# Another order of the same instructions in the six attention layers: feed-forward matmuls between scores and values on TensorE, query copy ahead of the exponentials, key scaling first on GpSimd

## What is computed

```python
for i in range(DEPTH):          # 6 layers
    x = attn_layer(shift_tokens(x), Wqkv[i], q_scale[i], k_scale[i], Wo[i]) + x
    x = ffn_layer(shift_tokens(x), ln_g[i], ln_b[i], W1[i], b1[i], W2[i], b2[i]) + x

# attn_layer
q, k, v = split(x @ Wqkv)                    # 128 -> 3 * 1024
q, k = l2norm(q) * qs, l2norm(k) * ksc       # per head of 64
q = q*cos*scale + rotate_half(q)*sin*scale   # k the same with 1/scale
sim = q @ k2.T * 8                           # own window of 32 keys and the one before
out = softmax(mask(sim)) @ v2
return out @ Wo                              # 1024 -> 128

# ffn_layer (hidden width 341)
a, gate = split(layernorm(x) @ W1 + b1)
return a * gelu(gate) @ W2 + b2
```

## Time and profile before

| | |
|---|---|
| median of three runs | 4083.23 us |
| the profiled execution | 4075.82 us |
| its span, first to last instruction | 4074.0 us |
| granted TensorE clock, mean | 0.976 |
| TensorE matmuls busy | 3730.5 us (92%) |
| VectorE busy | 3452.1 us (85%) |
| ScalarE busy | 3408.5 us (84%) |
| GpSimd busy | 2380.0 us (58%) |

### The profile page before, as it was taken

One profiled execution on the slowest core, in us unless ns is written; L12 is line 12 of the kernel. 1 busy time (PEld: TensorE's weight loads), 2 busy tenths in 40 slices (PEclk: granted clock), 3 DMA queues, 4 the chain that ended last, 5 costly groups with the idle time before them and its releaser, 6 DMA issues.

```text
span 4074.0 us, 125302 instructions
## 1 busy us (share of the span) xinstructions
PE 3730.5 (92%) x49248; PEld 2372.9 (58%) x49248; DVE 3452.1 (85%) x7192; ACT 3408.5 (84%) x9269; POOL 2380.0 (58%) x1420
## 2 busy tenths in 40 slices
PE   5999999967999999999999998999989999999997
PEld 2444444434666666666666666666666666666664
DVE  6999999957888888888878888888888888988884
ACT  3999999946888888888888888888888888888885
POOL 2434434436667666666666666666666666666662
PEclk8999999978999999999999999999999999999998
DMA  1000001002333333333333333333333333433332
GB/s 49 7 11 9 9 9 36 1 2 52 81 76 80 85 83 87 76 77 84 86 77 72 80 86 84 83 77 74 76 95 80 77 78 73 98 79 82 75 83 57
DMA packets 158791, 263.19 MB, mean 65 GB/s; under 512 B 45696, under 2 KB 72064, under 8 KB 157952
## 3 DMA queue, kind: packets, MB, share of 16 engines
q1 hardware_dynamic: 158208, 255.20, 26.6%
HBM read 26.43 MB, written 2.10 MB: 7 GB/s over the span
## 4 chain that ended last, share of the span: by engine, by line
PE 66%; ACT 13%; DVE 11%; issue 8%; POOL 1%; SPq 1%; DMA 1%; DVEq 0%; ACTq 0%; POOLq 0%
PE ps L655 18%; PE ps L724 7%; ACT arena L930 7%; PE ps L601 5%; PE ps L596 5%; PE ps L709 5%; PE ps L542 4%; PE ps L733 4%; PE ps L688 4%; PE ps L768 3%; PE ps L762 3%; PE ps L537 3%; DVE arena L1146 2%; PE ps L775 2%; ACT arena L917 2%
## 5 line engine op out<-in xcount | busy, mean ns | idle before, releaser
L655 PE MATMUL ps<-WB,arena 128*128 128x512 f32 x2304 | 1087.4, 606 | 46.9 <-ACT arena L946 27.0
L930 ACT ACTIVATE arena<-arena,nmx 128x64 f32<-128x64 f32 x3072 | 1022.1, 340 | 3.9 <-DVE arena L1221 3.3
L475 POOL TENSOR_TENSOR arena<-arena 128x1024 f32<-128x1024 f32 x192 | 455.2, 2371 | 476.0 <-DVE arena L1146 476.0
L655 PEld LDWEIGHTS ps<-WB,arena 128*128 128x128 f32 x2304 | 415.6, 193 | 471.8 <-issue 456.1
L484 POOL TENSOR_TENSOR arena<-arena,rr 128x1024 f32<-128x1024 f32 x192 | 367.3, 1913 | 524.7 <-DVE rr L1215 524.7
L1140 DVE TENSOR_TENSOR arena<-ps,tables 128x1024 f32<-128x1024 f32 x384 | 463.9, 1208 | 177.8 <-ACT arena L906 177.6
L906 ACT ACTIVATE arena<-ps 128x1024 f32<-128x1024 f32 x384 | 393.2, 1024 | 252.8 <-PE ps L655 247.1
L930 ACT ACTIVATION_READ_ACCUMULATOR arena<-arena,nmx 128x1 f32 x3072 | 594.5, 194 | 0.0
L724 PE MATMUL ps<-arena 128*64 128x64 f32 x12288 | 445.8, 231 | 117.4 <-issue 97.8
L724 PEld LDWEIGHTS ps<-arena 128*64 128x64 f32 x12288 | 409.4, 144 | 180.3 <-issue 168.8
L1146 DVE TENSOR_TENSOR arena<-ps,tables 128x512 f32<-128x512 f32 x768 | 489.5, 677 | 0.0
(11 more groups left out here) (109 smaller groups left out, 6482.1 us busy)
## 6 DMA issues: line engine op xcount, KB each, us to landing
arena<-arena SPq DMA_DIRECT2D x768, 128.0 KB, 2.3
arena<-arena SPq DMA_DIRECT2D x1536, 64.0 KB
WB<-wb SPq DMA_DIRECT2D x24, 512.0 KB, 4.6
arena<-X SPq DMA_DIRECT2D x384, 32.0 KB, 1.9
arena<-Y SPq DMA_DIRECT2D x96, 128.0 KB, 2.3
arena<-wa SPq DMA_DIRECT2D x8, 581.0 KB, 3.7
WF<-wf SPq DMA_DIRECT2D x6, 537.5 KB, 4.1
keep<-xT SPq DMA_DIRECT2D x1, 2048.0 KB, 7.8
```

Source lines behind the costliest of these rows:

```text
L475: pool.tensor_tensor(tu[:, K], t1[:, K], t2[:, K], ALU.add).then_inc(addk_r, 1)
L655: i = pe.matmul(banks[:, c, :], xs_[t % RING], WB[:, w * INNER + c * COL:w * INNER + (c + 1) * COL], start=True, stop=True)
L930: i = act.activation(pe3[:, :, h, :], sc[:, 64 * h:64 * h + 64].rearrange("p (k q) -> p k q", k=2), ACT.Exp, bias=nmx[:, h:h + 1], accum_o ...
```

## The change

The orders within the step are rewritten for TensorE, ScalarE, VectorE and GpSimd. No instruction is added or removed, and none changes its size. On TensorE the key transposes go between the projections of keys and queries, the query transposes ahead of the output projection, `scores` directly behind `values_of`, and `ff_back`, the first gate and value matmul, and `ff_down` between `scores` and `attend`. On ScalarE the copy of the turned keys goes between the two squares, and that of the turned queries ahead of all 16 exponentials; `ff_norm` stands ahead of the last GELU's place. On VectorE `norms` goes ahead of `ff_stats`, `masked` ahead of `inverse`, `ff_final` and `ff_hidden` are spread between them, and `ff_unit` goes behind `maxima`. On GpSimd `unit_k` goes ahead of `ff_rstd` and `probs_norm`. SyncE's order stays.

```diff
--- before.py
+++ after.py
@@ -505,12 +505,12 @@
                 if live(s + 1):
                     add_k(s + 1)
                     add_q(s + 1)
+                    unit_k(s + 1)
                 if chunk(s, 7) is not None:
                     ff_rstd(chunk(s, 7))
                 if live(s - 1):
                     probs_norm(s - 1)
                 if live(s + 1):
-                    unit_k(s + 1)
                     unit_q(s + 1)
 
 
@@ -779,24 +779,27 @@
             for s in range(-2, TILES + LAG):
                 if live(s + 1):
                     keys_of(s + 1)
+                if live(s):
+                    turn_k(s)
+                if live(s + 1):
                     queries_of(s + 1)
                 if live(s):
-                    turn_k(s)
+                    turn_q(s)
                 if live(s - 3):
                     output(s - 3)
                 if live(s):
-                    turn_q(s)
                     values_of(s)
+                if chunk(s, 7) is not None:
+                    ff_turn(s, chunk(s, 7))
+                if live(s):
+                    scores(s)
+                if chunk(s, 8) is not None:
+                    ff_back(s, chunk(s, 8))
+                if chunk(s, 9) is not None:
+                    ff_gate(s, chunk(s, 9), 0)
+                    ff_value(chunk(s, 9), 0)
                 if chunk(s, 10) is not None:
                     ff_down(s, chunk(s, 10))
-                if chunk(s, 7) is not None:
-                    ff_turn(s, chunk(s, 7))
-                if chunk(s, 9) is not None:
-                    ff_gate(s, chunk(s, 9), 0)
-                if live(s):
-                    scores(s)
-                if chunk(s, 9) is not None:
-                    ff_value(chunk(s, 9), 0)
                 if live(s - 2):
                     attend(s - 2)
                 if chunk(s, 9) is not None:
@@ -804,8 +807,6 @@
                     ff_value(chunk(s, 9), 1)
                     ff_gate(s, chunk(s, 9), 2)
                     ff_value(chunk(s, 9), 2)
-                if chunk(s, 8) is not None:
-                    ff_back(s, chunk(s, 8))
 
 
         @block.scalar
@@ -964,15 +965,15 @@
             for s in range(-2, TILES + LAG):
                 if live(s + 1):
                     square(s + 1, kv_ps, K, k_mm, sqk_r)
+                if live(s):
+                    turned_k(s)
+                if live(s + 1):
                     square(s + 1, q_ps, Q, q_mm, sqq_r)
                 if live(s):
-                    turned_k(s)
+                    turned_q(s)
                 if live(s - 1):
                     exponents(s - 1, range(0, 4))
                     exponents(s - 1, range(4, 8))
-                if live(s):
-                    turned_q(s)
-                if live(s - 1):
                     exponents(s - 1, range(8, 12))
                     exponents(s - 1, range(12, 16))
                 if chunk(s, 9) is not None:
@@ -983,10 +984,10 @@
                     ff_gelu(chunk(s, 9), 1)
                 if live(s):
                     values(s, 1)
+                if chunk(s, 8) is not None:
+                    ff_norm(chunk(s, 8))
                 if chunk(s, 9) is not None:
                     ff_gelu(chunk(s, 9), 2)
-                if chunk(s, 8) is not None:
-                    ff_norm(chunk(s, 8))
                 if live(s - 2):
                     outputs(s - 2)
                 if 0 < s + 1 < TILES:
@@ -1277,25 +1278,25 @@
                     residual(s - 3)
                 if live(s + 1):
                     sumsq(s + 1)
+                    norms(s + 1)
                 if chunk(s, 7) is not None:
                     ff_stats(chunk(s, 7))
-                if live(s + 1):
-                    norms(s + 1)
+                if chunk(s, 9) is not None:
+                    ff_hidden(chunk(s, 9), 0)
+                if live(s):
+                    masked(s)
+                if live(s - 1):
+                    inverse(s - 1)
+                if chunk(s, 9) is not None:
+                    ff_hidden(chunk(s, 9), 1)
                 if chunk(s, 10) is not None:
                     ff_final(chunk(s, 10))
+                if live(s):
+                    maxima(s)
                 if chunk(s, 9) is not None:
-                    ff_hidden(chunk(s, 9), 0)
-                if live(s - 1):
-                    inverse(s - 1)
-                if live(s):
-                    masked(s)
+                    ff_hidden(chunk(s, 9), 2)
                 if chunk(s, 7) is not None:
                     ff_unit(chunk(s, 7))
-                if chunk(s, 9) is not None:
-                    ff_hidden(chunk(s, 9), 1)
-                    ff_hidden(chunk(s, 9), 2)
-                if live(s):
-                    maxima(s)
                 q = chunk(s, 11)
                 if q is not None and q >= FF - NT // PER:
                     final(q)
```

## The result

The changed kernel takes 4047.61 us (median of 7 runs, 4042.57 to 4050.83), the kernel before 4080.06 us in the 7 runs beside it (4064.23 to 4088.86). The ratio is 0.9926, 95% interval 0.9908 to 0.9945: 0.7% faster, some 30 us. The forecast was 4097 us, slower. The time lies within the range, on the other side of no change, and a rival was nearest: "Program text wins", 4066 us, down to 4045. A ratio of 0.9926 with this interval is a gain clear of noise, though a small one.

A forecast was written before the change was run, and what follows sets the result against it. Each step was taken to have its own limit (TensorE's matmul sum in the gate step), plus waits for program text. Terms 18 - 24 - 4 + 18 + 5 = +13 us; forecast 4083 + 14 = 4097 us, range 4045 to 4132.

The forecast's parts named there:

- Program text wins: Rival, faster: stop relief reaches the back step too, `scores` gets no more stops; 4066 us, down to 4045; chance 0.28.
- First term: Plain down and turn steps: `turned_k` leaves the chain; 15.23 instead of 15.29 us, 13.91 instead of 13.93, -0.08 together.
- Fifth term: `scores` in down and gate steps: without `ff_down` and `ff_gate` ahead, stops for program text rise, +18 us.
- Fourth term: `attend`: matmuls between it and `scores` give program text time to come; -24 us in down steps, -4 in gate steps.
- relief in the back step: Rival's claim for `attend` in back steps: of 29.1 us of stops, 0.55 us of each goes, 12 us.
- Second term: Back step: `queries_of` waits 1.1 us for the later `ff_unit` instead of 0.28; +0.45 us a step.
- 40 us or more: Sign expected in the new profile: TensorE's total wait on the line of `ff_unit`, 9.1 us before.
- Third term: Gate step: `unit_k` ahead of `probs_norm` on GpSimd delays `unit_q`, so TensorE waits; +0.35 us a step.
- Sixth term: First step of each layer, bound by VectorE until `ff_unit`: `maxima` ahead costs 1.12 us, five times, +5 us.

## Why the prediction was wrong

**First term, the chain of the plain step: right.** 15.23 and 13.91 us were forecast, 15.26 and 13.90 came. Its last sentence was wrong: that the earlier query copy "makes `scores` ready sooner, for which nothing critical waits".

**Fifth term, stops in `scores` (+18 us): the step that failed.** They were to rise by 18 us and fell by 37.6. I took the number of instructions ahead of `scores` for the cause and the back step's row for its size. What the runs show in its place is the query copy. ScalarE's copy before and after, and TensorE's down step after, beside the earlier trace rows:

```profile
1538.98 1.00 ACT L922 ACTIVATE arena<-ps 128x1024 f32<-128x1024 f32 x1
1532.41 1.02 ACT L923 ACTIVATE arena<-ps 128x1024 f32<-128x1024 f32 x1
1535.76 1.61 PE L709 MATMUL ps<-arena 64*32 64x64 f32 x128
1537.30 2.84 PE L775 MATMUL ps<-arena,WF 128*128 128x512 f32 x6
```

Before, the copy ended at 1539.98 and `scores` started at 1540.78, behind the last matmul of `ff_down`: until 1539.98 TensorE's sequencer stood at the wait of `scores`, though the engine had work. Now the copy ended at 1533.43, 2.3 us ahead of `scores`, and the sequencer can run ahead into the next block of program text while the matmuls before it are still at work. The runs bear out that the copy decides: with it late, `scores` stops for 41.8 us (before), 41.3, 37.5 and 14.6 us; with it early, in all the others, for 2.6 to 5.7 us, whether `ff_down` stands ahead (3.4 us) or not.

The trace also holds the start of every packet of the instruction queue, and these show when a block is asked for. In the kernel before, at 20 of the 22 stops in `scores` the packet that the stop waited for started 1.04 to 1.84 us behind the end of the query copy (at the other two 0.14 and 0.37 us ahead of it); at the 165 places where `scores` went on into a new block without a stop, it had started 1.55 us or more ahead of the end of the copy. With the copy between the exponentials, all 7 packets started 1.13 to 1.49 us behind it. So a sequencer held at a wait asks for its next block late. What stays open is why the 14.6 us are so few: they fall only where `scores` starts 1 to 11 instructions behind the start of a block, and in the kernel before 1 to 56. Something else in the new TensorE order narrows that stretch.

**Fourth term, stops in `attend` (-28 us): the mechanism holds, but the term left out a second cause.** In down steps 26 stops became 3, in gate steps 8 became none, and taking `ff_down` out again costs 11 us, putting it in saves 15. In the kernel before, `ff_down` between leaves 3 of the down step's stops too. But the early copy, which the term did not weigh, also takes stops from `attend`: in the kernel before with turns and copies early they fall from 97.8 to 62.6 us in all, and 16 of the 26 in down steps are left. The rival's "relief in the back step" came as well: 23 stops became 11 (18 remain in turn steps, which were 23).

**Second term, the wait for `ff_unit` (+0.45 us a back step): right in place, mis-sized.** The plain back step is 15.68 us in the windows, not 14.97, and the wait is 61.4 us, which "40 us or more" allowed. `ff_unit` was to end 3.5 us behind the start of the back step (1562.1 against 1558.64) and ends 4.2 us behind it. The timeline after answers to the earlier trace rows:

```profile
1554.78 1.90 POOL L491 TENSOR_TENSOR arena<-arena,rinv 128x1024 f32<-128x1024 f32 x1 [2.03 <-DVE rinv L1195]
1555.96 0.75 DVE L1239 TENSOR_SCALAR ve<-mv 128x4 f32<-128x4 f32 x1
1556.13 1.95 PE L655 MATMUL ps<-WB,arena 128*128 128x512 f32 x4
1559.00 1.36 DVE L1244 TENSOR_SCALAR arena<-ps,mv,rstd 128x128 f32<-128x128 f32 x4
1560.51 1.96 PE L655 MATMUL ps<-WB,arena 128*128 128x512 f32 x4 [1.46 <-DVE arena L1244]
```

The epsilon addition started at 1555.96 and ended at 1556.71, with `unit_k`, which ended at 1556.68. I had written that `ff_stats` and `norms` "only change places". But `norms` starts `unit_k` on GpSimd, so the last small operation of `ff_stats` now falls beside it and is held until it ends; `masked`, `inverse`, `maxima` and `ff_unit` come 0.6 us later than they would. In the kernel with `tensor_reduce` the same place reads:

```profile
1554.05 1.90 POOL L493 TENSOR_TENSOR arena<-arena,rinv 128x1024 f32<-128x1024 f32 x1 [2.03 <-DVE rinv L1197]
1555.22 0.16 DVE L1241 TENSOR_REDUCE ve<-mve 128x4 f32<-128x8 f32 x1
1557.69 1.36 DVE L1246 TENSOR_SCALAR arena<-ps,mve,rstd 128x128 f32<-128x128 f32 x4
```

The reduction starts and ends while `unit_k` (1554.05 to 1555.95) still runs, and the plain back step, 15.10 us, is then near the forecast 14.97. The Trainium skill ("SBUF — State Buffer", section "Who interferes with whom") says that VectorE in a mode that uses its second port and GpSimd shut each other out for a whole instruction, which a `tensor_scalar` can run into, and that `tensor_reduce` never does on this chip. The 170, 754 and 161 ns agree; the prediction had not weighed this rule.

**Third term, `unit_q` (+0.35 us a gate step): the size by accident, the reason wrong.** The plain gate step rose by 0.30 us, but TensorE waited for `unit_q` only twice, 2.5 us in all. The gate step of before starts with

```profile
1573.16 3.60 PE L655 MATMUL ps<-WB,arena 128*128 128x512 f32 x8
1576.60 1.04 PE L688 MATMUL ps<-ident,arena 128*128 128x128 f32 x8
```

and now

```profile
1571.81 1.96 PE L655 MATMUL ps<-WB,arena 128*128 128x512 f32 x4 [0.84 <-ACT arena L947]
1573.60 1.04 PE L688 MATMUL ps<-ident,arena 128*128 128x128 f32 x8
1574.47 1.88 PE L655 MATMUL ps<-WB,arena 128*128 128x512 f32 x4
1576.32 1.10 PE L688 MATMUL ps<-ident,arena 128*128 128x128 f32 x8
```

From start to next start the eight projections took 3.44 us in one row; in two rows of four with the transposes between they take 1.79 + 1.85 = 3.64. By the medians of 46 gate steps that is +0.19 us, the value projections add 0.09 and the query transposes 0.06; `scores` takes 0.11 longer, which the matmuls behind it give back. What in the changed neighbours costs this was not tested. The wait for `unit_q` that I forecast is real only once `ff_unit` goes ahead of `maxima`.

**Sixth term (+5 us for five first steps)** was not told apart. **What the forecast didn't see at all:** `attend` waits 14.4 us more for DMAs, and the keys 15.0 us more for the value copy. Whether these stand where a stop for program text had been was not tested.

The sum: the forecast had -10 us for program text (-24, -4, +18) and +23 for the waits; their +13 on the median 4083.2 is 4096, the last line has 1 us more. Stops and the wait for the query copy fell by 128 us in the records, the other waits rose by 92, and the steps' means net to -28. That the time still lies in the range, near the rival's lower end of 4045, is luck: that end supposed a wait for `ff_unit` that costs nothing, while in fact it was longer than forecast and the stops in `scores`, which the rival left as they were, went.

## What to carry to other kernels

An early copy whose consumer "doesn't need it yet" can still pay, when an engine's sequencer stands at the wait for it and the program text behind is asked for late; look for "issue" stops inside rows of like instructions. When an edit moves an operation beside another engine's long one, do not keep its old duration: another form of instruction for the same sum can be free of the other engine (161 against 754 ns here). Parts of a reordering may each cost where the whole gains, so an ablation needs the partner edit (`ff_down` between: +74 us alone, -15 us with its partners).

## What the runs showed of the hardware

All of TensorE's records (weight loads, matmuls and the sequencer's) can be numbered in order. In the kernel before there are 97 gaps above 0.3 us within `scores` and `attend` in which TensorE ran neither a matmul nor a weight load and which end with one of their own matmuls or weight loads, not with a record of the sequencer's; all 97 fall on numbers that leave the same rest, 162, divided by 256. In the changed kernel there are 35, with the same rest. 100,588 records / 256 = 393 stands beside 392 packets of the instruction queue. At all 102 stops on such numbers in the kernel before, the instruction queue's packet had ended at least 1.21 us (median 1.40, at most 1.55) before TensorE went on; the packets themselves take 1.05 us by the median. So what a stop waits for includes over 1 us behind the transfer itself. By the same numbering a packet starts when TensorE has executed, by the median, 81 of the 256 records of the block ahead of the one that it brings (57 in the changed kernel), in single cases none yet, in others all 256. So the 57 instructions of one expectation above are a median and no fixed distance.
